# First attention pass: 64-row score tiles, a ring of three pairs of score banks, statistics of two interleaved heads per instruction

## What is computed

```python
qk = jnp.einsum('bhqd,bhkd->bhqk', Q, K)
scores = qk / math.sqrt(dk)
mean_sim = scores.mean(axis=(-2, -1))
max_sim = scores.max(axis=-1).mean(axis=-1)
probs = jax.nn.softmax(scores, axis=-1)
entropy_proxy = jnp.var(probs, axis=-1, ddof=1).mean(axis=-1)
feats = jnp.stack([mean_sim, max_sim, entropy_proxy], axis=-1)
```

## Time and profile before

| | us |
|---|---|
| median of three runs | 592.86 (592.42 to 593.71) |
| the profiled execution | 593.19 |
| its span, from the first to the last instruction | 591.4 |
| PE busy | 528.8 (89%) |
| DVE busy | 398.6 (67%) |
| ACT busy | 285.3 (48%) |
| POOL busy | 143.0 (24%) |

### The profile page before, as it was taken

The page is one execution under the profiler, slowest core; times in us unless marked ns, Lnnn a source line. Parts: engine busy times, 40 slices in busy tenths (PEclk is TensorE's granted clock), DMA queues, the critical chain, the costliest instruction groups (busy, mean ns, idle before and its releaser), DMA issues.

```text
span 591.4 us, 12949 instructions
## 1 busy us (share of the span) xinstructions
PE 528.8 (89%) x3952; PEld 412.8 (70%) x3952; DVE 398.6 (67%) x1306; ACT 285.3 (48%) x841; POOL 143.0 (24%) x376
## 2 busy tenths in 40 slices
PE   3899999897999969899999999778999999874996
PEld 1444444485566647788888888667999999762875
DVE  4389998966488974656656556547777877727553
ACT  0588989852565624342322223125665766732221
POOL 3232222110387771000121102120123322231000
PEclk9999999999899998899999999978999999996899
DMA  5900002001000000000000000000000000000001
GB/s 118 350 30 11 12 8 61 1 1 29 4 6 3 2 2 1 1 1 0 2 1 2 0 0 0 0 2 2 1 1 1 1 0 0 0 1 1 18 19 35
DMA packets 20447, 10.78 MB, mean 18 GB/s; under 512 B 7468, under 2 KB 18998, under 8 KB 20406
## 3 DMA queue, kind: packets, MB, share of 16 engines
q1 hardware_dynamic: 17750, 9.10, 5.5%
q10 hardware_dynamic: 2656, 1.18, 0.7%
HBM read 9.09 MB, written 1.18 MB: 17 GB/s over the span
## 4 chain that ended last, share of the span: by engine, by line
PE 76%; DVE 9%; issue 5%; ACT 4%; POOL 3%; DMA 1%; SPq 1%; DVEq 0%; POOLq 0%; ACTq 0%
PE psum L1225 10%; PE psum L1374 9%; PE psum L1179 6%; PE psum L1362 5%; PE psum L1363 5%; PE psum L1364 5%; PE psum L1415 4%; PE psum L1333 4%; PE psum L1446 4%; PE psum L1406 4%; PE psum L1426 3%; PE psum L1487 2%; PE psum L1212 2%; PE psum L1316 2%; PE psum L1474 1%
## 5 line engine op out<-in xcount | busy, mean ns | idle before, releaser
L569 ACT ACTIVATE work<-psum 128x512 f32<-128x512 f32 x64 | 38.1, 597 | 76.4 <-PE psum L1364 76.4
L500 ACT ACTIVATE wa<-psum,negmax 128x120 f32<-128x120 f32 x256 | 67.8, 376 | 10.5 <-DVE negmax L811 10.4
L1031 DVE TENSOR_TENSOR work<-psum,work 128x512 f32<-128x512 f32 x64 | 44.1, 691 | 31.4 <-PE psum L1364 25.5
L1225 PE MATMUL psum<-wa 32*128 32x480 f32 x128 | 63.1, 1082 | 2.1 <-ACT wa L500 2.0
L1374 PEld LDWEIGHTS psum<-dnT,work 128*128 128x128 f32 x512 | 62.0, 191 | 2.7
L1374 PE MATMUL psum<-dnT,work 128*128 128x128 f32 x512 | 62.3, 275 | 0.0
L597 ACT ACTIVATE work<-work,d 128x120 f32<-128x120 f32 x128 | 48.7, 381 | 21.7 <-DVE d L1103 21.7
L1041 DVE SCALAR_TENSOR_TENSOR x<-psum,gate,x 128x128 f32 (+1 forms) x128 | 36.1, 344 | 33.0 <-PE psum L1374 32.9
L1362 PE MATMUL psum<-x_hi,up_hi 128*128 128x512 f32 (+1 forms) x128 | 54.6, 426 | 2.6 <-DVE work L1031 2.3
L683 POOL TENSOR_TENSOR rstd<-mv,eps 128x1 f32<-128x1 f32 x32 | 6.1, 190 | 206.2 <-DVE mv L941 206.1
L1363 PE MATMUL psum<-x_lo,up_hi 128*128 128x512 f32 (+1 forms) x128 | 51.7, 404 | 0.0
(11 more groups left out here) (231 smaller groups left out, 1139.9 us busy)
## 6 DMA issues: line engine op xcount, KB each, us to landing
x<-in_x_dram ACTq DMA_DIRECT2D x4, 256.0 KB, 5.2
work<-in_L_ffn_w_down_dram SPq DMA_DIRECT2D x1, 1024.0 KB
wa<-mscratch SPq DMA_DIRECT2D x64, 2.0 KB
out_dram<-wa SPq DMA_DIRECT2D x4, 256.0 KB, 2.3
wa<-in_ctx_dram SPq DMA_DIRECT2D x16, 60.0 KB, 1.8
work<-in_L_xattn_Wq_dram SPq DMA_DIRECT2D x1, 512.0 KB
work<-in_L_xattn_Wk_dram SPq DMA_DIRECT2D x1, 512.0 KB
work<-in_L_xattn_Wv_dram SPq DMA_DIRECT2D x1, 512.0 KB
```

What stands on the lines that cost most here:

```text
L500: e = nc.scalar.activation(prob[:, z, hh, :], psum[:, 3 + 2 * half + h // 4, (h % 4) * LK:(h % 4 + 1) * LK], ACT.Exp, bias=negmax[:, z, hh ...
L1031: nc.vector.tensor_tensor(hT[:, e % 2, j, :], psum[:, 2 * j, :], silu[:, j, :], ALU.mult).then_inc(c_h, 1)
L1225: m = nc.tensor.matmul(psum[:, 3 + g, 0:4 * LK], qs[rows, z, :], kexp[rows, z].rearrange("p i k -> p (i k)"), start=True, stop=True)
```

## The change

Five things change.

- **Score tiles.** `kexp` has 8 copies of k's columns instead of 4 (`halfscale`, each with one head of 8 in each half of the partitions), so POOL's instruction writes 960 columns instead of 480. A score matmul now has 64 rows: rows 0 to 63 and 64 to 127 for each half, still 480 columns and one bank each. Half 0 holds heads 0 to 3 and 8 to 11, half 1 the others. The number of matmuls and of columns is the same.
- **Bank ring.** v moves from bank 2 into bank 1. The halves take the bank pairs 2-3, 4-5, 6-7 in turn, so a half waits for the exponentials three halves back instead of two. Bank 7 is now a score bank, so the 16 small matmuls into it wait for the last exponential.
- **Statistics.** `bn_stats` runs on two neighbouring heads at once: 240 elements, ordered key by key with the two heads alternating. The even elements are then one head and the odd ones the other.
- **End of the statistics.** Since each part is already a whole head, the merge has fewer instructions.
- **Loops.** PE, DVE and ACT have the pass written out in full (`peel=NB`); POOL and SP keep theirs.

```diff
+HALF_ROWS = HALF0 * DK0
+SCORE_RING = 3
@@ shape_constants
+    halfscale = (part // DK0 % HALF0 == np.arange(HALF0)[None, :]).astype(np.float32) / math.sqrt(DK0)
@@ build
-        kexp = wa[:, 0:960].rearrange("p (z i k) -> p z i k", z=2, i=GROUP0)
+        kexp = wa[:, 0:1920].rearrange("p (z i k) -> p z i k", z=2, i=HALF0)
+        def score_bank(b, half):
+            return 2 + (2 * b + half) % SCORE_RING * 2
+
+        def heads_of(half):
+            return [HALF0 * g + 4 * half + i for g in range(2) for i in range(4)]
@@ ACT a_values
-                nc.scalar.copy(v0[:, b, :], psum[0:LK, 2, 0:D]).then_inc(a_v, 1)
+                nc.scalar.copy(v0[:, b, :], psum[0:LK, 1, LQ + LK:LQ + LK + D]).then_inc(a_v, 1)
@@ POOL a_expand
-                nc.gpsimd.tensor_tensor(kexp[:, z], kT[:, b, :].unsqueeze(1).to_broadcast([P, GROUP0, LK]),
-                                        groupscale.unsqueeze(2).to_broadcast([P, GROUP0, LK]), ALU.mult
+                nc.gpsimd.tensor_tensor(kexp[:, z], kT[:, b, :].unsqueeze(1).to_broadcast([P, HALF0, LK]),
+                                        halfscale.unsqueeze(2).to_broadcast([P, HALF0, LK]), ALU.mult
@@ DVE a_stats
-                    for h in range(half * HALF0, (half + 1) * HALF0):
-                        s = nc.vector.bn_stats(bnout[:, bass.ds(b * H0 + h, 1), :].rearrange("p a s -> p (a s)"),
-                                               prob[:, z, h, :])
+                    for h in heads_of(half)[::2]:
+
+                        s = nc.vector.bn_stats(
+                            bnout[:, bass.ds(b * HALF0 + h // 2, 1), :].rearrange("p a s -> p (a s)"),
+                            prob[:, z, h:h + 2, :].rearrange("p h k -> p k h"))
@@ PE a_scores
-                    if not isinstance(b, int) or b >= 1:
-                        pe.wait_ge(a_exp, b * 2 + half - 1)
-                    for g in (2 * half, 2 * half + 1):
-                        rows = slice(GROUP_ROWS * g, GROUP_ROWS * (g + 1))
-                        m = nc.tensor.matmul(psum[:, 3 + g, 0:4 * LK], qs[rows, z, :],
-                                             kexp[rows, z].rearrange("p i k -> p (i k)"), start=True, stop=True)
+                    if 2 * b + half >= SCORE_RING:
+                        pe.wait_ge(a_exp, 2 * b + half - SCORE_RING + 1)
+                    for g in range(2):
+                        rows = slice(HALF_ROWS * g, HALF_ROWS * (g + 1))
+                        m = nc.tensor.matmul(psum[:, score_bank(b, half) + g, 0:4 * LK], qs[rows, z, :],
+                                             kexp[rows, z, 4 * half:4 * half + 4].rearrange("p i k -> p (i k)"),
+                                             start=True, stop=True)
@@ PE after the pass
             pe.wait_ge(ld_w, 16 * N_W)
+            pe.wait_ge(a_exp, 2 * NB)
...
             m.then_inc(l1_pe, 1)
-            pe.wait_ge(a_exp, 2 * NB)
```

More of the change, by code:

```diff
@@ L78, in software_pipeline @@
 def software_pipeline(eng, stages, n=NB, peel=4):
-    assert all(lag <= peel - 2 for lag, _ in stages) and (n - peel) % 2 == 0
+    assert peel == n or all(lag <= peel - 2 for lag, _ in stages) and (n - peel) % 2 == 0
     def step(b, parity):
@@ L89, in software_pipeline @@
         step(b, b % 2)
-    with eng.Fori(0, (n - peel) // 2) as i:
-        for parity in range(2):
-            step(i * 2 + (peel + parity), parity)
+    if n > peel:
+        with eng.Fori(0, (n - peel) // 2) as i:
+            for parity in range(2):
+                step(i * 2 + (peel + parity), parity)
     for b in range(n, n + peel):
@@ L497, in run @@
                         reused(act, a_bn, b, 2)
-                    for h in range(HALF0):
-                        hh = half * HALF0 + h
+                    for h, head in enumerate(heads_of(half)):
                         e = nc.scalar.activation(
-                            prob[:, z, hh, :], psum[:, 3 + 2 * half + h // 4, (h % 4) * LK:(h % 4 + 1) * LK],
-                            ACT.Exp, bias=negmax[:, z, hh:hh + 1])
+                            prob[:, z, head, :], psum[:, score_bank(b, half) + h // 4, (h % 4) * LK:(h % 4 + 1) * LK],
+                            ACT.Exp, bias=negmax[:, z, head:head + 1])
                     e.then_inc(a_exp, 1)
@@ L811, in run @@
                     nc.vector.tensor_reduce(
-                        negmax[:, z, half * HALF0:(half + 1) * HALF0].rearrange("p (a h) -> p a h", a=2),
-                        psum[:, 3 + 2 * half:5 + 2 * half, 0:4 * LK].rearrange("p a (h k) -> p a h k", k=LK),
+                        negmax[:, z, :].rearrange("p (a c h) -> p a c h", a=2, c=2)[:, :, half],
+                        banks(score_bank(b, half), 2)[:, :, 0:4 * LK].rearrange("p a (h k) -> p a h k", k=LK),
                         AX_X, ALU.max, negate=True).then_inc(a_neg, 1)
@@ L833, in _ @@
             dve.wait_ge(a_bn, 2 * NB)
-            mean_e, m2_e, mean_o, m2_o = (bnout[:, :, i] for i in (1, 2, 4, 5))
-            HALF_KEYS = LK // 2
-            nc.vector.tensor_tensor(small[:, 0, :], mean_e, mean_o, ALU.add)
-            nc.vector.tensor_tensor(small[:, 1, :], mean_e, mean_o, ALU.subtract)
+            stats = bnout.rearrange("p r (j s) -> p r j s", j=2)
+            of_pairs = lambda i: small[:, i, :].rearrange("p (r j) -> p r j", j=2)
+            nc.vector.tensor_tensor(of_pairs(2), stats[:, :, :, 1], stats[:, :, :, 1], ALU.mult)
             nc.vector.tensor_tensor(small[:, 5, 0:NB], qsum[:, :], ksum[:, :], ALU.mult).then_inc(f_dve, 1)
             dve.wait_ge(f_dve, 1)
-            nc.vector.tensor_tensor(small[:, 2, :], small[:, 0, :], small[:, 0, :], ALU.mult)
-            nc.vector.tensor_tensor(small[:, 3, :], small[:, 1, :], small[:, 1, :], ALU.mult)
+            nc.vector.reciprocal(small[:, 0, :], small[:, 2, :])
             nc.vector.tensor_tensor(small[:, 4, :].rearrange("p (b h) -> p b h", b=NB),
@@ L846, in _ @@
             dve.wait_ge(f_dve, 2)
[L847 to L855 removed]
+            nc.vector.scalar_tensor_tensor(out=of_pairs(2), in0=stats[:, :, :, 2],
+                                           scalar=1.0 / ((LK - 1) * LK ** 2), in1=of_pairs(0),
                                            op0=ALU.mult, op1=ALU.mult).then_inc(f_dve, 1)
@@ L1213, in a_project @@
                 nc.tensor.matmul(psum[:, 1, LQ:LQ + LK], w4T[:, 1, :], xc[:, z, LQ:LQ + LK], start=True, stop=True)
-                nc.tensor.matmul(psum[0:LK, 2, 0:D], xc[:, z, LQ:LQ + LK], w4T[:, 2, :], start=True, stop=True
+                nc.tensor.matmul(psum[0:LK, 1, LQ + LK:LQ + LK + D], xc[:, z, LQ:LQ + LK], w4T[:, 2, :], start=True, stop=True
                                  ).then_inc(a_qkv, 1)
```

22 lines of the change are left out of this document (7 added, 15 removed).

## The result

| | median, us | runs | against before |
|---|---|---|---|
| before, same chip | 593.29 | 592.42 to 594.15 | |
| after | 586.81 | 585.81 to 587.97 | 0.9892 [0.9867, 0.9916] |

The change made the kernel faster by 6.5 us, 1.1%. The prediction was 603.0 us with a range of 595 to 612, so the time lies outside it, on the other side of before. Rival A had named 586.1 us.

A forecast was written before the change was run, and what follows sets the result against it. PE bounds the kernel before; DVE was to bound the changed one at 6.42 us a step. Small matmuls start at 125.5 instead of 115.57, +9.9 us on 593.19, less 0.33: 602.8, given as 603.0, range 595 to 612.

The forecast's parts named there:

- Rival A: Whole pass: interleaved read costs nothing and the clock rises, ACT bounds at 5.3 us a step, 586.1 us; chance 0.15.
- What bounds the kernel now: First pass: PE alone sets the pace at 1.2 GHz, 5.97 us a step; DVE could do 5.38, ACT 5.2 to 5.3.
- Statistics: DVE's bn_stats: one interleaved 240-element instruction costs 0.50 us (bounds 0.31 to 0.56), so DVE's step becomes 6.42 us.
- Score tiles: PE's score halves: 1.90 us at 1.2 GHz, 1.06 at 2.4 GHz; either way PE stays under DVE's 6.42 us a step.
- rival C: PE's score matmuls: two 64-row products don't run side by side, a step takes 9.2 us, near 644 us; chance 0.04.
- POOL's expansion: POOL in the pass: grows from 0.99 to about 2.0 us a step, made two steps before its use, costs nothing.
- Ring and loops: Score banks and written-out pass: a third bank pair gains nothing under a DVE bound; written-out loops were put at nothing.
- The moved wait: End of the pass: the 16 small matmuls start behind the last exponentials, +3.35 us at an unchanged pass.
- Rival A's own sum: End of pass: step times at ACT's 5.3 us put the small matmuls at 108.8, 6.8 us earlier: 586.1 us; chance 0.15.

The follow-up runs named there:

- experiment on the read: The changed kernel with 45 instructions added at the end of DVE's program, reading 240 elements in different patterns; bn_stats took 0.31 to 0.49 us each.
- the fastest version: The changed kernel with the 16 small matmuls waiting only for the exponentials two halves before the last: 579.49 us, 580.33 us the second time.

## Why the prediction was wrong, step by step

**What bounds the kernel now: right.** PE alone, at 1.2 GHz. Lighter statistics alone moved nothing, and with 32-row tiles the changed kernel showed the same chain, 5.97 us a step. DVE's own pace of 5.38 us was measured as 5.38 and 5.40 in the changed kernel with the old statistics, ACT's 5.2 to 5.3 as 5.15.

**Statistics: the step that failed.** "I take 0.50, the value of the nearest row, since both leave a contiguous run at every element." It measured 0.31, the low end of its own bounds. The row was real but it wasn't near in what counts: its elements lie in ever new places, while the new source goes back and forth between two runs, each contiguous in itself. With 0.50 the forecast had DVE as the bound at 6.42 us a step; a step took 5.15 us, with ACT as the bound. The experiment on the read separates the two: two streams 0.31, four streams 0.46, every sixth element 0.48. The Trainium skill, page "Advanced Engine Details and Errata", section "Memory Cachelines", had been weighed with both readings; the measured prices fit the one in which both lines stay open, for two streams but not for four. With this one number put in and the clock risen, the prediction's own sum is rival A. The chance of 0.15 on it was too low: a term between 0.31 and 0.56, on which the sign hung at 0.41, and which no row of its kind priced, deserved something nearer to even odds. And the range stopped at 595, although the low bound of that term together with a risen clock led to 586; it left out the case that took place.

**Score tiles: right.** 1.06 us a half was predicted for 2.4 GHz and 1.07 measured; 1.94 for 1.2 GHz, and 1.97 measured. They run side by side; rival C fell. In the forecast this was worth nothing, since either clock was under DVE's 6.42; with that price gone it is the part that matters most, 595.19 us without it for 586.81 and 586.18. That the clock would rise was in rival A, reasoned from which row groups work, and the runs with 32 and 64 rows bear it out. That it falls again within the pass wasn't foreseen. The Trainium skill, page "TensorE: Matmul & The Clock Gate", Part 1, has sustained PE work lift the clock; by that rule the run with 32-row tiles, 80.00 us busy of 80.00, should have risen, and it didn't.

**POOL's expansion: right in the pass, wrong at its end.** 1.79 us for the 2.0 predicted, hidden as long as it is two steps ahead. At the end of the pass, with the wait taken away, it is a link of the chain.

**Ring and loops: right for this change.** The ring of two gave 586.44 for 586.81 and 586.18, the loops 0.9 us inside the spread. At the very end of the pass the ring may be worth about 1 us. The loops were put at nothing from the spacing of the statistics in written-out steps; with tiles and the old statistics, steps at the turn of the loop lasted 5.90 us and more for 5.37, so that held only with the lighter statistics.

**The moved wait: right.** 3.35 us predicted; the small matmuls take 6.96 us, as said, and putting them back ahead of the wait starts them 2.9 to 5.3 us earlier with three bank pairs and 3.6 with two, where the medians differ by 3.5. With three pairs the medians differ by 6 to 7 us, of which the wait explains only that part. So of the 13 us by which the fastest version beats before, the moved wait took back some 3 to 5.

**Rival A's own sum: right to 0.7 us, in part by luck.** The small matmuls came at 107.2 instead of 108.8, 1.6 us better, and the part behind the pass gave 1.9 us back, which no term held.

## What to carry to other kernels

A price taken from the nearest row holds only if the row is near in what makes the cost: here that was the order in which addresses follow one another, not whether they are neighbours. Where one disputed term spans the sign of the whole, the chances should be near even and the range should reach both ends. When a change has parts, ask of each which engine it takes off the path: lighter DVE work was worth nothing until PE's clock rose, and 6.3 us after, or 1.2 to 1.9 where the loops were written out as well; and a wait that moved with a resource (bank 7) was the first thing to look at once the rest had worked.

## What the runs showed of the hardware

- DVE reads two streams of fp32 in turn at the price of one (0.31 us for 240 elements), four streams at 0.46, eight at 0.49. A distance of 8 bytes is free (0.31), and 16, 24 and 32 bytes cost 0.48 to 0.49. A sum of two operands pays the same as `bn_stats`.
- TensorE was busy for 80.00 of 80.00 us in steps whose score matmuls, 3.80 of 5.97 us, are fp32 products of 32 rows, two at a time, and by its durations it stayed at 1.2 GHz. With the same columns in pairs of 64 rows it rose to 2.4 GHz at 26.3 us, after 2.30 of 2.30 us busy from 24.00 on. In one profile it then fell to 1.2 GHz for about a third of the time from 43.4 on: PE had been busy for 4.54 of 6.81 us before a fall and for 3.41 of 3.41 before a rise. In another it stayed at 2.4 GHz for 54.40 us, in which PE was busy for 33.06. These rows don't say why it fell.
- Where the trace has no clock record, the column shows 1.00. Only durations told that this was 1.2 GHz; the same instruction at two levels (score half 1.97 and 1.07 us) is the reliable reading.
